# Edge MLP of a four-layer graph network: edge attributes from a three-part bf16 split to unsplit fp32 on the four row groups of TensorE

## Chip, cores and metric

One Trainium2 chip, one of its cores. The metric is the device time of one execution in microseconds (us). The kernel before takes 4524.12 us (median of 3 runs, 4523.55 to 4528.85).

## What is computed

A network of four graph layers over 3125 nodes (128 features) and 50000 edges sorted by target node. The change lies in the edge part of the last layer:

```
ef = jnp.concatenate([x[row], x[col], edge_attr], axis=-1)      # 50000 x (128 + 128 + 32)
h = jax.nn.relu(ef @ W1 + b1)                                   # 256 wide
h = jax.nn.relu(h @ W2 + b2)                                    # 256 wide
edge_out = h @ W3 + b3
aggr = jax.ops.segment_sum(edge_out, col, num_segments=x.shape[0])
```

W1 is used in three pieces: for the source node (its product is a table in DRAM, from which rows are gathered), for the target node (its product is the tile XR, kept as three bf16 parts whose sum is the fp32 value), and for the 32 edge attributes. W3 is applied after the sum over the edges, so the kernel only sums the second relu's result by target node.

## The kernel before

The edges are cut into tiles of 128 edges that share one block of 128 target nodes; four tiles are a quad, and there are 104 quads (QUADS). `mlp_edges` (L1073) runs over the quads in one block of five instruction streams. `in_quads` (L1105) writes out the first four and the last steps and loops over the rest, four steps to an iteration. The order of work is written by hand: each engine's `step` says what it does for which quad, and semaphores tie the engines together.

TensorE's step q (L1190) does, in this order:

- `first(q+1)` (L1150): for each of the four tiles j, three bf16 matmuls of 256 columns (L1158), which pick the target node's row with the 0/1 matrix hot_t, and two bf16 matmuls of 256 columns (L1161) for the edge attributes. It first reads four block numbers into registers (L1100), since L1158's operand address depends on them. Sums go to H1, PSUM banks 0 and 1.
- `second(q)` (L1164): eight fp32 matmuls of 256 columns (L1169), each of which is two instructions in the profile, into H2, banks 4 and 5.
- `turn(q+1)` (L1172): eight transposes of 128 columns (L1177) into T, banks 2 and 3.
- `summed(q-1)` (L1180): eight fp32 matmuls of 128 columns (L1187), two instructions each, into O, banks 6 and 7.

VectorE's step q (L1298): `taken(q-2)` adds O to the accumulator, four instructions (L1296); `added(q+1)` adds the gathered source rows to H1 (L1265), 1024 elements wide; `make_hot_t(q+2)` (L1256, L1258); `rest_parts(q+2)` (L1271); `make_hot(q)` (L1281); `low_parts(q+2)` (L1277); `shifted(q)` adds the bias to H2 (L1288). ScalarE's step q: `high_parts(q+2)` (L1219), `middle_parts(q+2)` (L1223), the relu of T for quad q+1 (L1232), the relu of quad q (L1236). GpSimd gathers the source rows with four indirect DMAs a quad (L1144), into four buffers. SyncE loads, a quad at a time, the targets (L1125, 128 KB) and the four tiles of edge attributes (L1130, 64 KB each).

The edge attributes e (32 numbers) come from DRAM four times over, on 128 partitions: copies 0 and 1 are turned into the bf16 high part, copy 2 into the middle part, copy 3 into the low part. L1219 rounds all four copies to bf16, L1271 subtracts for copies 2 and 3, L1223 rounds what is left, L1277 subtracts again for copy 3. The weights are split alike, once, by GpSimd at the end of `quad_lists` (L1400 to L1416), which runs long before, ahead of the third layer. Two bf16 matmuls over 128 rows then give the product of the split values.

`first(q)` waits for `ea_split` (L1277 of this quad), `hot_t_done` and `h1_added` (L1265 of quad q-1, which frees H1). `turn(q)` waits for `h1_added` of its quad and for `h1_done` (L1232) of the quad before, which frees T.

The third layer (`gine_edges`, L938) already uses fp32 matmuls over 32 rows for the same attributes, four tiles on partitions 0-31, 32-63, 64-95 and 96-127, with their sums in four banks (L1004, 128 columns each).

Of the kernel before, what the change touches and what calls it, by code (L numbers as in the profile page):

```python
# [20 lines left out]
BF16 = mybir.dt.bfloat16  # L21
# [61 lines left out]
def build(nc, t):  # L83

    with ExitStack() as ctx:
# [3 lines left out]
        def sem(name):  # L89
            return ctx.enter_context(nc.semaphore(name))  # L90
# [62 lines left out]
        wrow_all = sb("wrow", [P, 2, GROUP_EDGES], BF16)  # L153
        wrow = wrow_all[0:SPLIT * SPLIT, :, :]
# [918 lines left out]
        def mlp_edges(target):  # L1073
# [14 lines left out]
            ea_hi, ea_rest, ea_mid, ea_split = (sem(f"mlp_ea_{k}") for k in ("hi", "rest", "mid", "split"))  # L1088
            rest = sm[:, 1, :]
            ea_parts = neg  # L1090
# [28 lines left out]
            with nc.Block() as block:  # L1119
                @block.sync  # L1120
                def _(sp):
                    def load(q, r):
# [26 lines left out]
                def _(e):  # L1149
                    def first(q, r):  # L1150
                        s = r % 2
                        blocks = parts_of(mybir.EngineType.PE, q, SUBS)
                        e.wait_ge(ea_split, q + 1)
                        e.wait_ge(hot_t_done, q + 1)
                        wait(e, h1_added, q)
                        for j in range(SUBS):
# [3 lines left out]
                            for k in range(2):  # L1160
                                last = e.matmul(H1[:, j, :], ea_parts[:, s, j * P:(j + 1) * P], edge_w[k], start=False, stop=(k == 1))  # L1161
# [28 lines left out]
                    def step(q, r, k):  # L1190
                        if is_quad(q + 1):
                            first(q + 1, (r + 1) % 4)
# [21 lines left out]
                def _(a):  # L1214
                    def high_parts(q, r, turn):
                        s = r % 2
                        a.wait_ge(ea_in[s], ea_before + 16 * SUBS * (turn + 1))
                        wait(a, h1_ready, q - 1)
                        a.activation(ea_parts[:, s, :], ea_all[:, s, :], ACT.Copy).then_inc(ea_hi, 1)  # L1219

                    def middle_parts(q, r):
                        a.wait_ge(ea_rest, q + 1)
                        a.activation(ea_parts[2 * EDGE_D:, r % 2, :], rest[2 * EDGE_D:, :], ACT.Copy).then_inc(ea_mid, 1)  # L1223

                    def step(q, r, k):
                        if is_quad(q + 2):
# [12 lines left out]
                    high_parts(0, 0, 0)  # L1239
                    middle_parts(0, 0)  # L1240
# [5 lines left out]
                def _(v):  # L1246
# [19 lines left out]

                    def rest_parts(q, r):
                        s = r % 2
                        v.wait_ge(ea_hi, q + 1)
                        wait(v, ea_split, q)  # L1270
                        v.tensor_tensor(rest[2 * EDGE_D:, :], ea_all[2 * EDGE_D:, s, :], ea_parts[2 * EDGE_D:, s, :], ALU.subtract).then_inc(ea_rest, 1)  # L1271

                    def low_parts(q, r):
                        low = ea_parts[3 * EDGE_D:, r % 2, :]
                        v.wait_ge(ea_mid, q + 1)
                        v.wait_ge(ea_rest, q + 1)
                        v.tensor_tensor(low, rest[3 * EDGE_D:, :], low, ALU.subtract).then_inc(ea_split, 1)  # L1277
# [20 lines left out]
                    def step(q, r, k):  # L1298
# [9 lines left out]
                        if is_quad(q + 2):  # L1308
                            low_parts(q + 2, (r + 2) % 4)
# [4 lines left out]
                    rest_parts(0, 0)  # L1314
                    low_parts(0, 0)
# [4 lines left out]

        edge_w = [wrow_all[:, k, 0:HID] for k in range(2)]
# [40 lines left out]
        def quad_lists():  # L1362
# [8 lines left out]
            edge_w_split = sem("edge_w_split")  # L1371
            w_rest = pm[:, 0, 0:HID]
            w_hi, w_mid, w_lo = (pm[:, 1, k * P:(k + 1) * P].bitcast(BF16) for k in range(SPLIT))
# [7 lines left out]
            def pool_also(pool):  # L1381
# [18 lines left out]
                n = [0]  # L1400

                def step(ins):
                    n[0] += 1
                    ins.then_inc(edge_w_split, 1)
                    pool.wait_ge(edge_w_split, n[0])
# [498 lines left out]
```

## Time and profile before

| | |
|---|---|
| median of 3 runs | 4524.12 us (4523.55 to 4528.85) |
| the profiled execution | 4522.14 us, span of its instructions 4520.3 us |
| edge MLP, about | 3510 to 4425 us of the span |
| busy over the whole span | PE 76%, PEld 59%, DVE 59%, ACT 36%, POOL 63% |

PE is TensorE's matmuls, PEld its weight loads, DVE VectorE, ACT ScalarE, POOL GpSimd, SPq and PEq the instruction queues of SyncE and TensorE. In a row of the timeline, the first number is the start in us from the span's beginning, the second the time from the start of the group's first instruction to the end of its last, xN the number of instructions; in square brackets the idle time of the engine before it and what ended it. Matmuls overlap: one of 256 columns lasts about 0.27 us, but in an unbroken stream the next one starts 0.11 us after it. "Issue" is time for which the profile shows no other engine to wait for. The granted clock (PEclk) is 1.00 at 2.4 GHz and 0.50 at 1.2 GHz.

### The profile page before, as it was taken

How to read it: one execution, taken by the hardware profiler on the slowest of the kernel's cores; microseconds unless marked ns; L12 is line 12 of the kernel's file. 1: busy time of each engine (PE TensorE's matmuls, PEld its weight loads, DVE VectorE, ACT ScalarE, POOL GpSimd, SP SyncE). 2: the span in 40 equal slices, each digit the busy share in tenths (PEclk: the TensorE clock that was granted, in tenths of full speed). 3: DMA queues.
4: the chain of work that ended last, by engine and by line, in shares of the span. 5: the costliest groups of instructions: out<-in, count | busy, mean ns of one | idle time of the engine just before them, and what ended most of it. 6: DMA issues, size and time to landing. Idle time of an engine off the chain costs nothing. (4 is left out here: it accounts for less than half of the span.)

```text
span 4520.3 us, 91957 instructions
## 1 busy us (share of the span) xinstructions
PE 3424.3 (76%) x20700; PEld 2666.3 (59%) x20793; DVE 2652.9 (59%) x6184; ACT 1615.5 (36%) x3137; POOL 2825.8 (63%) x2944
## 2 busy tenths in 40 slices
PE   6999999967777755555655555555556799999997
PEld 3777777745555534444444444444444688898894
DVE  5888888866666653333333333333334788888885
ACT  3666666645555531111211111211113333333334
POOL 4555555537777758888678888588884444444440
PEclk7999999979999965555555555655556899999998
DMA  3333333313223212222122222122221333333330
GB/s 113 92 100 100 99 99 100 101 48 80 80 80 80 79 50 59 58 58 59 47 68 59 58 59 59 55 60 58 59 59 48 108 110 110 106 110 109 106 101 15
DMA packets 293253, 349.80 MB, mean 77 GB/s; under 512 B 63537, under 2 KB 236756, under 8 KB 292916
## 3 DMA queue, kind: packets, MB, share of 16 engines
q0 software_dynamic: 98528, 229.12, 17.9%
q1 hardware_dynamic: 140481, 92.05, 7.5%
q10 hardware_dynamic: 54162, 27.77, 2.2%
q8 instruction: 24, 0.39, 0.0%
q14 instruction: 58, 0.47, 0.0%
HBM read 332.61 MB, written 16.07 MB: 77 GB/s over the span
## 5 line engine op out<-in xcount | busy, mean ns | idle before, releaser
L988 POOL DMA_INDIRECT gath<-source_rows_narrow,gine_idx x1176 | 1136.7, 967 | 386.2 <-issue 316.1
L1038 DVE TENSOR_TENSOR vs<-psum,gath 128x512 f32<-128x512 f32 x366 | 253.1, 692 | 1027.7 <-SPq L973 954.0
L1004 PE MATMUL psum<-gine_lin,ea 32*128 32x128 f32 x2928 | 288.4, 483 | 749.3 <-DVE vs L1038 721.7
L1144 POOL DMA_INDIRECT gath<-source_rows,idx_all x416 | 430.3, 1034 | 509.5 <-DVE vs L1265 352.8
L760 POOL DMA_INDIRECT gath<-source_rows,idx_all x488 | 465.1, 953 | 377.2 <-PE psum L807 262.3
L1004 PEld LDWEIGHTS psum<-gine_lin,ea 32*128 32x128 f32 x2928 | 183.8, 297 | 849.9 <-DVE vs L1038 778.7
L760 POOL DMA_INDIRECT gath<-source_rows_narrow,idx_all x488 | 462.8, 948 | 206.1 <-issue 136.6
L790 PE MATMUL psum<-lk,att_b 128*128 128x512 f32 x732 | 375.2, 619 | 113.8 <-DVE lk L885 113.2
L1068 ACT ACTIVATE pm<-vs 128x512 f32<-128x512 f32 x186 | 117.2, 630 | 811.1 <-DVE vs L1038 806.6
L807 PEld LDWEIGHTS psum<-gath,pt 128*128 128x128 f32 x2928 | 365.1, 192 | 36.8 <-DVE zsum L918 1.8
L1013 PE MATMUL psum<-hot,pm 128*128 128x128 f32 x1488 | 363.4, 421 | 20.4 <-ACT pm L1068 19.4
L1169 PE MATMUL psum<-weight_all,pm 128*128 128x256 f32 x1664 | 377.2, 380 | 0.0
L1068 ACT ACTIVATE sm<-vs 128x512 f32<-128x512 f32 x180 | 113.4, 630 | 716.8 <-DVE vs L1038 637.0
L807 PE MATMUL psum<-gath,pt 128*128 128x128 f32 x2928 | 366.4, 275 | 0.9 <-ACT pt L844 0.8
L1013 PE MATMUL psum<-lk,sm 128*128 128x128 f32 x1440 | 358.2, 427 | 1.0 <-ACT sm L1068 1.0
L1013 PEld LDWEIGHTS psum<-hot,pm 128*128 128x128 f32 x1488 | 312.0, 310 | 64.4 <-DVE ACC L1047 45.8
L885 DVE SCALAR_TENSOR_TENSOR lk<-vs 128x512 f32<-128x512 f32 x366 | 253.5, 693 | 159.5 <-DVE vs L881 149.5
L1013 PEld LDWEIGHTS psum<-lk,sm 128*128 128x128 f32 x1440 | 308.4, 316 | 42.7 <-ACT sm L1068 21.7
L1169 PEld LDWEIGHTS psum<-weight_all,pm 128*128 128x128 f32 x1664 | 308.7, 191 | 39.0
L820 ACT ACTIVATE vs<-psum 128x512 f32<-128x512 f32 x366 | 205.4, 595 | 288.9 <-PE psum L772 288.9
L844 ACT ACTIVATE pt<-psum 128x512 f32<-128x512 f32 x366 | 205.5, 595 | 268.6 <-PE psum L799 261.7
L894 DVE CUSTOM_DVE_ANT_0 sm<-psum,neg 128x512 f32<-128x512 f32 x366 | 245.0, 687 | 92.7 <-PE psum L790 91.7
(243 smaller groups left out, 6412.2 us busy)
## 6 DMA issues: line engine op xcount, KB each, us to landing
rel<-rel_rows SPq DMA_DIRECT2D x244, 128.0 KB
ea<-in_edge_attr_tiles SPq DMA_DIRECT2D x416, 64.0 KB
ea<-in_edge_attr ACTq DMA_DIRECT2D x366, 64.0 KB
gath<-source_rows_narrow,gine_idx POOLq DMA_INDIRECT x1176
gath<-source_rows,idx_all POOLq DMA_INDIRECT x904
rel<-quad_rel_rows SPq DMA_DIRECT2D x104, 128.0 KB
gath<-source_rows_narrow,idx_all POOLq DMA_INDIRECT x488
source_rows<-ACC SPq DMA_DIRECT2D x12, 512.0 KB, 2.9
```

The lines of the kernel that those rows point to most:

```text
L760: pool.indirect_dma_start(out=gath[:, i % 4, j, 0:width], out_offset=None, in_=dram, in_offset=bass.IndirectOffsetOnAxis(ap=idx_all[:, i, ...
L790: e.matmul(S[h], att_b[:, att[h], :], lk[:, h, :], start=True, stop=True).then_inc(s_ready, 1)
L807: last = e.matmul(O[h], pt[:, h, j, :], gath[:, s4, j, h * D:(h + 1) * D], start=(j == 0), stop=(j == SUBS - 1))
L885: v.scalar_tensor_tensor(lk[:, h, :], vs[:, h, :], 0.2, vs[:, h, :], ALU.mult, ALU.max).then_inc(leaked, 1)
L894: v.tensor_tensor_reduce(out=sm[:, h, :], in0=S[h], in1=neg[:, s, :], scale=1.0, scalar=-4 * MASK, op0=ALU.subtract, op1=ALU.max, accum_ou ...
L988: pool.indirect_dma_start(out=ring[:, g % RING, j, :], out_offset=None, in_=table1, in_offset=bass.IndirectOffsetOnAxis(ap=gine_idx[:, g, ...
L1004: last = e.matmul(E[:, j, :], ea[rows, s, :], gine_lin[rows, layer, :], start=True, stop=True)
L1013: last = e.matmul(O[s4], pms[s4][:, j * P:(j + 1) * P], hots[s4][:, j, :], start=(j == 0), stop=(j == SUBS - 1))
L1038: v.tensor_tensor(vs[:, s, :].rearrange("p (j d) -> p j d", j=SUBS), E, ring[:, bass.ds(slot, 1), :, :].rearrange("p a j d -> p (a j) d"), ...
L1068: a.activation(pms[s4], vs[:, s, :], ACT.Relu).then_inc(gi["msg"], 1)
L1144: pool.indirect_dma_start(out=gath[:, q % 4, j, :], out_offset=None, in_=table, in_offset=bass.IndirectOffsetOnAxis(ap=quad_idx[:, q, j:j ...
L1169: last = e.matmul(H2[:, j, :], h1[:, h, j * P:(j + 1) * P], w2[h], start=(h == 0), stop=(h == 1))
```

## The change

The edge attributes are loaded once, tile j on partitions 32j to 32j+31, 16 KB each, and are used in fp32 as they are. Their matmul is over 32 rows, on row group j of the array, 256 columns wide, with the fp32 weights, four to a quad (eight instructions, since an fp32 matmul is two), after all twelve matmuls with XR. The four steps of the split on ScalarE and VectorE and the split of the weights on GpSimd go. H1 and T are laid out anew: tile j has bank j, its first half for H1 and its second half for T, so `first` now waits for `h1_done` of the quad before in place of `h1_added`. ScalarE's relu reads T in the new order and writes h1 as before, through another view. SyncE's load of the attributes waits for `h1_ready` (first of the quad two before) in place of `ea_hi` and `ea_rest`. TensorE itself waits for the attributes' DMA, between the two groups of matmuls.

```diff
-            H1 = psum[:, 0:2, :].rearrange("p a n -> p (a n)").rearrange("p (j d) -> p j d", d=HID)
-            T = psum[:, 2:4, :].rearrange("p a n -> p (a n)").rearrange("p (h n) -> p h n", h=2)
+            H1 = psum[:, 0:SUBS, 0:HID]
+            T = psum[:, 0:SUBS, HID:2 * HID].rearrange("p j (h n) -> p j h n", h=2)
...
+            ea_tiles = ea_all[:, :, 0:P]
+            h1_by_tile = pm[:, :, :].rearrange("p h (j n) -> p j h n", j=SUBS)
...
-                        wait(sp, ea_hi, q - 1)
-                        wait(sp, ea_rest, q - 1)
+                        wait(sp, h1_ready, q - 1)
                         for j in range(SUBS):
-                            sp.dma_start(ea_all[:, s, j * P:(j + 1) * P],
+                            sp.dma_start(ea_tiles[EDGE_D * j:EDGE_D * (j + 1), s, :],
...
-                    def first(q, r):
+                    def first(q, r, turn):
                         s = r % 2
                         blocks = parts_of(mybir.EngineType.PE, q, SUBS)
-                        e.wait_ge(ea_split, q + 1)
                         e.wait_ge(hot_t_done, q + 1)
-                        wait(e, h1_added, q)
+                        wait(e, h1_done, q)
                         for j in range(SUBS):
                             for k in range(SPLIT):
                                 e.matmul(H1[:, j, :], hot_t[...], XR[...], start=(k == 0), stop=False)
-                            for k in range(2):
-                                last = e.matmul(H1[:, j, :], ea_parts[:, s, j * P:(j + 1) * P], edge_w[k], start=False, stop=(k == 1))
+                        e.wait_ge(ea_in[s], ea_before + 16 * SUBS * (turn + 1))
+                        for j in range(SUBS):
+                            rows = slice(EDGE_D * j, EDGE_D * (j + 1))
+                            last = e.matmul(H1[:, j, :], ea_tiles[rows, s, :], edge_w1[rows, :], start=False, stop=True)
                         last.then_inc(h1_ready, 1)
...
-                                last = e.transpose(T[:, h, j * P:(j + 1) * P], h1e[:, j, h * D:(h + 1) * D], ident)
+                                last = e.transpose(T[:, j, h, :], h1e[:, j, h * D:(h + 1) * D], ident)
...
-                            high_parts(q + 2, (r + 2) % 4, 2 * k + (r + 2) // 2)
-                            middle_parts(q + 2, (r + 2) % 4)
...
-                            a.activation(h1[:, :, :], T, ACT.Relu).then_inc(h1_done, 1)
+                            a.activation(h1_by_tile, T, ACT.Relu).then_inc(h1_done, 1)
...
-                            rest_parts(q + 2, (r + 2) % 4)
...
-                            low_parts(q + 2, (r + 2) % 4)
...
-                step(pool.tensor_copy(w_hi, edge_w1[:, :]))
-                step(pool.tensor_tensor(w_rest, edge_w1[:, :], w_hi, ALU.subtract))
-                step(pool.tensor_copy(w_mid, w_rest))
-                step(pool.tensor_tensor(w_lo, w_rest, w_mid, ALU.subtract))
-                pool.memset(edge_w[1], 0.0).then_inc(edge_w_split, 1)
...
-                    pool.tensor_copy(edge_w[to][rows, :], part[rows, :]).then_inc(edge_w_split, 1)
```

## Rows read from the trace of the kernel before

**Rows 1.** Busy time of each engine by stretch of the span (also clock, DMA share, GB/s).

```profile
3600.00:3800.00 200.00, 198.04 (x1426) 179.52 (x1425) 168.28 (x261) 77.06 (x96) 97.41 (x95) 1.00 0.39 110
```

**Rows 2.** Timeline of TensorE over one quad's step.

```profile
3907.30 0.54 PE L1158 MATMUL psum<-XR,hot_t 128*128 x3
3907.67 0.38 PE L1161 MATMUL psum<-wrow,neg 128*128 128x256 bf16 x2
3907.89 0.49 PE L1158 MATMUL psum<-XR,hot_t 128*128 x3
...
3909.52 3.62 PE L1169 MATMUL psum<-weight_all,pm 128*128 128x256 f32 x16
3912.98 1.04 PE L1177 MATMUL psum<-consts,vs 128*128 128x128 f32 x8
3913.85 1.95 PE L1187 MATMUL psum<-hot,TMP 128*128 128x128 f32 x16
3916.13 0.41 PE L1158 MATMUL psum<-XR,hot_t 128*128 x2 [0.33 <-issue]
```

**Rows 3.** Timeline of VectorE, ScalarE and SyncE's queue around the same step.

```profile
3905.14 1.90 SPq L1130 DMA_DIRECT2D ea<-in_edge_attr_tiles  x4
...
3905.70 1.03 ACT L1232 ACTIVATE pm<-psum 128x1024 f32<-128x1024 f32 x1 [0.58 <-PE psum L1177]
...
3907.61 2.12 DVE L1296 TENSOR_TENSOR ACC<-ACC,psum 128x256 f32 x4 [0.45 <-PE psum L1187]
...
3909.78 1.23 DVE L1265 TENSOR_TENSOR vs<-psum,gath 128x1024 f32<-128x1024 f32 x1
```

**Rows 4.** Timeline, third layer: one group of four fp32 matmuls over 32 rows.

```profile
1738.71 0.50 PE L1004 MATMUL psum<-gine_lin,ea 32*128 32x128 f32 x8 [0.62 <-DVE vs L1038]
```

**Rows 5.** The same instructions as a group, 1738.5 to 1739.5 us: ns min/median/max.

```profile
L1004 PE MATMUL psum<-gine_lin,ea x8: 270/321/372, 1738.7 to 1738.9; 32*128 32x128 f32 x8
```

**Rows 6.** The same line from 2500 to 2560 us, at clock 0.50.

```profile
L1004 PE MATMUL psum<-gine_lin,ea x104: 416/496/578, 2503.1 to 2556.6; 32*128 32x128 f32 x104
```

**Rows 7.** Timeline of the second layer's XR: 3-row and 128-row matmuls in turn.

```profile
966.23 0.28 PE L482 MATMUL psum<-bias_rows,ones_rows 3*128 3x128 bf16 x1
...
966.44 0.80 PE L480 MATMUL psum<-weight_all,XT 128*128 128x128 f32 x2
967.16 0.10 PEld L482 LDWEIGHTS psum<-bias_rows,ones_rows 3*128 3x128 bf16 x1 [0.23 <-issue]
```

**Rows 8.** Timeline, second layer: a 9-row matmul between 128-row ones.

```profile
1209.41 0.38 PE L780 MATMUL psum<-wrow,we_parts 9*128 9x512 bf16 x1
1209.73 0.82 PE L782 MATMUL psum<-hot_t,XR 128*128 128x512 bf16 x3
```

**Rows 9.** Busy time of each engine by stretch, for the clock of two stretches.

```profile
966.00:974.00 8.00, 8.00 (x28) 4.92 (x26) 2.58 (x4) 2.23 (x4) 6.17 (x7) 0.50 0.21 59
1738.50:1739.50 1.00, 0.50 (x8) 0.31 (x8) 0.45 (x2) 0.63 (x1) 0.94 (x1) 1.00 0.20 66
```

**Rows 10.** Timeline at the end of the stage that splits the weights.

```profile
1649.46 3.02 POOL L1415 COPY wrow<-pm 32x256 bf16<-32x256 bf16 x6
...
1635.38 15.96 SPq L290 DMA_DIRECT2D source_rows_narrow<-TMP  x7
```

**Rows 11.** Timeline of the first quads of the edge MLP.

```profile
3538.68 0.35 DVE L1256 TENSOR_SCALAR hot_t<-rel,consts 128x512 bf16<-128x512 bf16 x1
...
3542.01 0.82 PE L1158 MATMUL psum<-XR,hot_t 128*128 x3 [15.58 <-DVE neg L1277]
...
3546.57 1.22 DVE L1265 TENSOR_TENSOR vs<-psum,gath 128x1024 f32<-128x1024 f32 x1 [4.71 <-PE psum L1161]
...
3551.02 0.82 PE L1158 MATMUL psum<-XR,hot_t 128*128 x3 [2.08 <-DVE neg L1277]
...
3560.38 0.49 PE L1158 MATMUL psum<-XR,hot_t 128*128 x3
3560.58 1.03 ACT L1232 ACTIVATE pm<-psum 128x1024 f32<-128x1024 f32 x1 [1.43 <-PE psum L1177]
```

More of the change, by code:

```diff
@@ L152, in build @@
         rel = sb("rel", [P, 2, GROUP_EDGES], BF16)
-        wrow_all = sb("wrow", [P, 2, GROUP_EDGES], BF16)
-        wrow = wrow_all[0:SPLIT * SPLIT, :, :]
+        wrow = sb("wrow", [SPLIT * SPLIT, 2, GROUP_EDGES], BF16)
         gath = sb("gath", [P, 4, SUBS, 2 * D])
@@ L1083, in mlp_edges @@
             count_turned, count_copied, count_summed, count_done = (sem(f"mlp_count_{k}") for k in ("turned", "copied", "summed", "done"))
-            H1 = psum[:, 0:2, :].rearrange("p a n -> p (a n)").rearrange("p (j d) -> p j d", d=HID)
-            T = psum[:, 2:4, :].rearrange("p a n -> p (a n)").rearrange("p (h n) -> p h n", h=2)
+            H1 = psum[:, 0:SUBS, 0:HID]
+            T = psum[:, 0:SUBS, HID:2 * HID].rearrange("p j (h n) -> p j h n", h=2)
             H2 = psum[:, 4:6, :].rearrange("p a n -> p (a n)").rearrange("p (j d) -> p j d", d=HID)
             O = psum[:, 6:8, :].rearrange("p a n -> p (a n)").rearrange("p (j h n) -> p j h n", j=SUBS, h=2)
-            ea_hi, ea_rest, ea_mid, ea_split = (sem(f"mlp_ea_{k}") for k in ("hi", "rest", "mid", "split"))
-            rest = sm[:, 1, :]
-            ea_parts = neg
+            ea_tiles = ea_all[:, :, 0:P]
             h1e = vs[:, :, :].rearrange("p a n -> p (a n)").rearrange("p (j d) -> p j d", d=HID)
             h1 = pm
+            h1_by_tile = pm[:, :, :].rearrange("p h (j n) -> p j h n", j=SUBS)
             h2a = TMP[:, 0:8, :].rearrange("p a d -> p (a d)").rearrange("p (j d) -> p j d", d=HID)
@@ L1191, in step @@
                         if is_quad(q + 1):
-                            first(q + 1, (r + 1) % 4)
+                            first(q + 1, (r + 1) % 4, 2 * k + (r + 1) // 2)
                         if is_quad(q):
@@ L1214, in _ @@
                 def _(a):
[L1215 to L1223, printed above, removed]
                     def step(q, r, k):
-                        if is_quad(q + 2):
-                            high_parts(q + 2, (r + 2) % 4, 2 * k + (r + 2) // 2)
-                            middle_parts(q + 2, (r + 2) % 4)
                         if is_quad(q + 1):
@@ L1238, in _ @@
                     target.scalar(a)
-                    high_parts(0, 0, 0)
-                    middle_parts(0, 0)
                     in_quads(a, step)
@@ L1265, in added @@
                         v.tensor_tensor(h1e, H1, gath[:, r, :, :], ALU.add).then_inc(h1_added, 1)
[L1267 to L1277, printed above, removed]
                     def make_hot(q, r):
@@ L1313, in _ @@
                     make_hot_t(0, 0, 0)
-                    rest_parts(0, 0)
-                    low_parts(0, 0)
                     in_quads(v, step)
@@ L1318, in _ @@
                     v.tensor_copy(stat[:, 0, :], psum[:, 2, 0:NODE_BLOCKS]).then_inc(count_done, 1)
-        edge_w = [wrow_all[:, k, 0:HID] for k in range(2)]
         def quad_places():
@@ L1370, in quad_lists @@
             rel_b = rel[0:QUADS, 0, :]
-            edge_w_split = sem("edge_w_split")
-            w_rest = pm[:, 0, 0:HID]
-            w_hi, w_mid, w_lo = (pm[:, 1, k * P:(k + 1) * P].bitcast(BF16) for k in range(SPLIT))
             def sp_also(sp):
@@ L1399, in pool_also @@
                 pool.dma_start(quad_rel_rows, rel_b).then_inc(rel_stored, 16)
[L1400 to L1405, printed above, removed]
-                step(pool.tensor_copy(w_hi, edge_w1[:, :]))
-                step(pool.tensor_tensor(w_rest, edge_w1[:, :], w_hi, ALU.subtract))
-                step(pool.tensor_copy(w_mid, w_rest))
-                step(pool.tensor_tensor(w_lo, w_rest, w_mid, ALU.subtract))
-                pool.memset(edge_w[1], 0.0).then_inc(edge_w_split, 1)
-                pool.wait_ge(edge_w_split, 5)
-                for k, (to, at, part) in enumerate(((0, 0, w_hi), (0, 1, w_mid), (0, 2, w_hi), (0, 3, w_hi), (1, 0, w_lo), (1, 2, w_mid))):
-                    rows = slice(EDGE_D * at, EDGE_D * (at + 1))
-                    pool.tensor_copy(edge_w[to][rows, :], part[rows, :]).then_inc(edge_w_split, 1)
-                pool.wait_ge(edge_w_split, 11)
                 pool.wait_ge(rel_stored, 16)
@@ L1881 @@
         "edge_weight": padded(a["edge_weight1"][:, 0], 0).reshape(GROUPS, GROUP_EDGES),
-        "edge_attr_tiles": np.tile(padded(a["edge_attr_32"], 0).reshape(TILES, P, EDGE_D).transpose(0, 2, 1), (1, P // EDGE_D, 1)),
+        "edge_attr_tiles": padded(a["edge_attr_32"], 0).reshape(TILES, P, EDGE_D).transpose(0, 2, 1),
         "edge_attr": padded(a["edge_attr_32"], 0).reshape(GROUPS, SUBS, P, EDGE_D).transpose(0, 1, 3, 2).reshape(GROUPS, SUBS * EDGE_D, P),
```

1 line of the change is left out of this document (removed).

## Prediction, made before the changed kernel ran

> **What bounds the kernel now.** I read the table by stretches first. In the middle of the edge MLP TensorE's matmuls are busy for 198 of 200 us at the full granted clock, VectorE for 168, GpSimd for 97, ScalarE for 77 [rows 1]. So the question is what the change does to TensorE's stream; work taken from the others counts only where they hold TensorE up.
>
> The timeline of one step gives that stream [rows 2]. `first` starts at 3907.30, `second` at 3909.52, `turn` at 3912.98, `summed` at 3913.85, the next `first` at 3916.13: 2.22, 3.46, 0.87 and 2.28 us, the last with 0.33 us in which nothing came. Those 0.33 stand at the back edge of the loop, once in four quads, and none of it is a wait for the split of the attributes. A stage's length is its instruction count times a spacing: in `second` 16 instructions in 3.46 us, 0.216 each for 256 columns in fp32. In `first` there are 20 bf16 instructions of 256 columns. Three in a row take 0.49 us from first start to last end and two take 0.38, so one more costs 0.11. Only the first three of a quad stand wider: 0.37 us to the fourth, 0.123 each, against 0.32 for the three from 3907.89 on. These are the L1158 ones, whose address comes from a register; I read it as TensorE's queue handing them out one by one, while a quad's first have no lead.
>
> The rest has room. ScalarE's relu of T ends at 3905.70 + 1.03 = 3906.73, 0.57 before `first` starts [rows 2, 3]. VectorE ends its four sums at 3909.73 and begins `added` at 3909.78, when H1 is ready; it ends at 3911.01, 1.97 before `turn` wants it [rows 2, 3].
>
> **What the change removes.** Per quad: eight bf16 matmuls of 0.11, 0.87 us of TensorE; two VectorE and two ScalarE instructions of 512 columns, which hide behind TensorE today and so give nothing. After them VectorE has less to do than before in every step, and what is late next is TensorE again. On GpSimd the weight split goes; its last copies end at 1652.48, while SyncE's last store is only issued at 1651.34 and has yet to land before the stage can end [rows 10]. I give it 0 (between -1 and 0).
>
> **What it adds on TensorE, per quad.** Eight fp32 instructions over 32 rows and 256 columns, two rounds on four row groups. The third layer has the same form with 128 columns. At clock 1.00 its eight take 0.50 us from first start to last end [rows 4, 9]; the eight one after another would take 7 x 0.108 + 0.27 = 1.03. The longest lasts 372 ns, the shortest 270 [rows 5]. That fits a first weight load of 0.10 in the open, two rounds 0.11 apart, 0.02 for the four starts and 0.27 for the last (0.10 + 0.11 + 0.02 + 0.27 = 0.50). So four row groups do run side by side, and a round of 256 columns costs 0.216: two make 0.43, plus 0.02.
>
> The price of going between 128-row and 32-row matmuls is in two places. A 3-row matmul in turn with fp32 ones over 128 rows, at clock 0.50 [rows 7, 9]: from its start at 966.23 to the next load at 966.44 is 0.21, of which 128 bf16 columns at 1.2 GHz stream for 0.107, so 0.10 on the way back. From there to the next 3-row load at 967.16 is 0.72: two fp32 instructions of 128 columns stream 0.43, their first load stands open for 0.16 (the longest less the shortest at this clock, 578 - 416 ns, [rows 6]), 0.13 is left for the way in. No weight load starts ahead: TensorE's load row shows 0.23 us idle. At clock 1.00 a 9-row matmul of 512 columns starts at 1209.41 and the 128-row one 0.32 later; the next of these come at (0.82 - 0.38) / 2 = 0.22, so the way back costs 0.10 at full clock too [rows 8]. I take 0.12 in and 0.10 back, and an open load of 0.10 after each: 0.42 a quad. Bounds: 0, were all of it hidden, and 0.60, were both ways and both loads as at half the clock (0.13, 0.16, 0.10, 0.16, and a rounding up).
>
> One rule speaks against the change: by the Trainium skill, TensorEngine Tiling (Array Packing), Key Properties, a change of tiling mode (not of tile alone) drains TensorE. By this rule two drains a quad are paid, and the trace agrees with 0.12 and 0.10; without the rule the sum below would be 0.22 a quad less.
>
> **What it moves.** The twelve XR matmuls now come in one row, with no L1161 between them. Today the L1161 pairs let the queue catch up; without them the 0.123 to 0.13 of a quad's first three [rows 2] may hold for all twelve. Bounds 12 x 0.108 = 1.30 and 12 x 0.13 = 1.56; I take 1.50, nearer to the row that has no lead. TensorE's own wait for the attributes' DMA comes after them; its target is worked out from a register, an instruction of the same kind as those in between, and I hide it under the way in. SyncE's four loads today go out at 3905.14 and take 1.90 to issue [rows 3]; the new wait lets them go when `first` of two quads before ends, near 3909.5, and they are wanted two steps, 16 us, later. The next `rel` load queues behind them and moves by under half a us, with as much to spare. They carry 16 KB in place of 64.
>
> `first` now waits for the relu of T, not for `added`. In a full step the relu is 0.57 us early, and `summed` lies between. Behind that wait are `second`, `turn` and `summed`, so a late relu would move everything; I take 0. The relu of T itself becomes a read of four half banks of the same 1024 elements, at 1.03.
>
> Sum for `first`: 1.50 + 0.12 + 0.10 + 0.43 + 0.02 + 0.10 + 0.10 = 2.37, against 2.22: **+0.15 us**. For the 102 quads in the full stream +15.3.
>
> **The start.** The first `first` begins at 3542.01, after the split of quad 0; its other input, hot_t, ended at 3539.03 [rows 11]. Put 0.15 behind it, it starts at 3539.18, 2.8 earlier. At clock 0.50 it is some 0.5 shorter (eight instructions of 0.213 go, 0.85 of rounds and some 0.4 of changes come), so `added(0)` moves from 3546.57 to 3543.2. Then 1.22, the transposes 1.04 and the relu 1.03, with three hand-overs: 3546.8 for the second `first`, against 3551.02, which waited for the split of quad 1: -4.2. The third `first` follows the transposes at once today (3560.38), before the relu at 3560.58 has run; in this step there is no `summed` yet, so the new wait costs 3561.61 + 0.15 - 3560.38 = 1.4. Start: -2.8 (between -5 and 0, as the clock falls).
>
> **Total:** +15.3 - 2.8 = +12.5. The profiled execution took 4522.14, 2.0 under the median: 4534.6 for it, some 4537 for a median. A measurement of this kernel can tell about 0.2%, 9 us, from no change.
>
> **Rivals.**
>
> *The row groups win (faster).* Place: between the last XR matmul and `second`. If the loads of the new mode are fetched ahead and nothing drains, and the twelve keep 0.108, `first` is 1.30 + 0.43 + 0.02 = 1.75: -0.47 a quad, -48 and -3 at the start, 4473. For it: the clean 0.50 for eight in the third layer [rows 4]. Against: rows 7 and 8, where no load is early. It decides once pacing and changes together cost under 0.41 where I reckon 0.62 (0.20 and 0.42): then `first` is 0.06 shorter than today and the sum, with the start, is -9. Chance 0.11, and 0.04 more for part of it.
>
> *The pacing does not hold (no change).* With 1.30 for the twelve `first` is 2.17 to 2.20: -0.03 a quad, -3 and -3: 4518 to 4522. For it: all later threes stand at 0.11 today. Against: they have a lead then. Chance 0.20.
>
> *The relu is late (slower by more).* From 0.57 us later on, each 0.1 costs 10 us. It might come from ScalarE's order or a slower read across four banks; 0.3 past the point gives 4567. ScalarE loses two instructions, which speaks against. Chance 0.05.
>
> *The row groups don't run together,* so that the change doesn't do what it says: 8 x 0.216 = 1.73 in place of 0.43, +133: 4670. Against: rows 4. Its one difference is that sums are added to what H1 holds, not begun. Chance 0.04.
>
> *My forecast:* 0.56, by itself 4528 to 4550, some 0.10 of it within 9 us of no change.
>
> Slower: 0.46 + 0.05 + 0.04 = 0.55. No change: 0.10 + 0.20 = 0.30. Faster: 0.11 + 0.04 = 0.15. The range takes in the second rival and half of the gap to the first (4505), and upwards the 0.60 for changes and 1.56 for pacing, (0.18 + 0.06) x 102 = +24 more (4560); it leaves out the first rival and the last two.
>
> **What would show it.** In the profile after: `first` from its first L1158 to the first L1169 at 2.37 plus an open load, which shows as L1169's first matmul longer than its others; the twelve at 0.124, end of the last to the first 32-row load some 0.1 with TensorE's load row idle; eight 32-row matmuls in about 0.7 from first start to last end; `second`, `turn` and `summed` at 3.46, 0.87 and 1.79 as before; VectorE at about 6.3 us a quad, waiting for TensorE before L1265 or L1288; the second `first` some 8 us behind the first, no longer 9. The forecast is wrong if the twelve take 1.30, if loads start before the last XR matmul has ended, or if TensorE sits idle before L1158 for the relu in each step.

## The result, and the profile after

| | before | after |
|---|---|---|
| median of the runs, us | 4523.84 (4522.45 to 4529.80, 6 runs) | 4543.34 (4543.04 to 4546.34, 6 runs) |
| the profiled execution, us | 4522.14 | 4543.88 |
| its span, us | 4520.3 | 4542.1 |
| mean granted clock of TensorE | 0.797 | 0.795 |

The changed kernel is slower: ratio 1.0041, with an interval of 1.0028 to 1.0054, or +19.5 us. The forecast was 4537 in a range of 4505 to 4560. Three single executions in these rounds took 5259 to 6786 us (two of the kernel before, one of experiment 2), and the ratios leave them out, while the medians have them in.

TensorE is still the engine without room. The first fence is the middle stretch of the edge MLP as in [rows 1] (us, then busy us and instructions of PE, PEld, DVE, ACT and POOL; clock, DMA share, GB/s). VectorE is at 131 of 200 us instead of 168, ScalarE at 45 instead of 77, and TensorE stays at 198 with fewer instructions, 1400 for 1426:

```profile
3600.00:3800.00 200.00, 198.20 (x1400) 166.56 (x1399) 131.37 (x210) 45.49 (x47) 88.54 (x93) 1.00 0.31 84
```

The timeline of one step, which answers to [rows 2, 3]:

```profile
3908.13 1.02 ACT L1217 ACTIVATE pm<-psum 128x1024 f32<-128x1024 f32 x1 [6.48 <-PE psum L1175]
...
3909.72 1.67 PE L1154 MATMUL psum<-XR,hot_t 128*128 x12
...
3910.03 2.12 DVE L1267 TENSOR_TENSOR ACC<-ACC,psum 128x256 f32 x4 [1.55 <-PE psum L1185]
...
3911.32 0.71 PE L1159 MATMUL psum<-edge_w,ea 32*128 32x256 f32 x8
3911.97 3.72 PE L1167 MATMUL psum<-weight_all,pm 128*128 128x256 f32 x16
...
3912.16 1.23 DVE L1248 TENSOR_TENSOR vs<-psum,gath 128x1024 f32<-128x1024 f32 x1
...
3915.53 1.04 PE L1175 MATMUL psum<-consts,vs 128*128 128x128 f32 x8
```

`first` now takes 3911.97 - 3909.72 = 2.25 us, `second` 3915.53 - 3911.97 = 3.56. Before they were 2.22 and 3.46: the step is 0.13 longer. The twelve L1154 matmuls last 1.67 from first start to last end; one lasts 0.28, so their starts stand (1.67 - 0.28) / 11 = 0.126 apart. The eight of 32 rows take 0.71. `second` is 0.10 longer for its first weight load, which stands open. The weight loads of the same step:

```profile
3909.72 1.49 PEld L1154 LDWEIGHTS psum<-XR,hot_t 128*128 128x128 bf16 x12
3911.32 0.31 PEld L1159 LDWEIGHTS psum<-edge_w,ea 32*128 32x128 f32 x8
3911.97 3.32 PEld L1167 LDWEIGHTS psum<-weight_all,pm 128*128 128x128 f32 x16 [0.33 <-issue]
```

No load of L1167 starts before the last 32-row matmul has streamed: 0.33 us of idle load row. The first matmul behind it shows this as its length. In the group of these matmuls over two steps (ns, min/median/max) the longest is 483 where before it was 382:

```profile
L1167 PE MATMUL psum<-weight_all,pm x32: 379/379/483, 3903.5 to 3915.3; 128*128 128x256 f32 x32
```

Who waits for whom, from 3565 to 4430 (us in total, times, longest):

```profile
DVE ACC L1267 <- PE psum L1185: 163.1, 100, 2.0
DVE TMP L1259 <- PE psum L1167: 63.3, 100, 0.8
PEld psum L1167 <- issue: 33.5, 101, 0.3
...
PE psum L1154 <- issue: 6.6, 23, 0.4
PE psum L1154 <- ACT pm L1217: 1.3, 1, 1.3
```

VectorE waits for TensorE in each step. TensorE waits for the relu of T once, in the third quad, and never in the steady stream.

**Where the 21.8 us between the two spans lie.** The edge MLP begins with the memset of its accumulator; in the trace before it starts at 3533.3, after at 3543.0:

```profile
L1231 DVE MEMSET ACC<- x1: 5392/5392/5392, 3543.0 to 3543.0; 128x6400 f32 x1
```

From there to the end it is 987.0 before and 999.1 after, +12.1. The edge MLP is not all of that: from the memset to the end of its last sums it is 901.3 before and 910.1 after, **+8.9 us in the edge MLP** by the unrounded times, and what follows it takes 85.8 before and 88.9 after, **+3.1 behind it**. The diff changes nothing behind it. Over all the traces of this study that last stretch takes 85.8 to 90.5 us, the shortest at a granted clock of 0.86 and the longest at 0.78; here the clock is 0.86 before and 0.81 after. The other **+9.8 us stand ahead of it**, where the diff has nothing but the removed split of the weights and the smaller buffer and input. The third layer's gathers are the group that grew there. From the first to the last it took 3449.0 - 1654.4 = 1794.6 us before; the same rows give 3460.9 - 1657.2 = 1803.7 after, 9.1 more. First of before (L988), then of after (L987), duration in ns as min/median/max:

```profile
L988 POOL DMA_INDIRECT gath<-source_rows_narrow,gine_idx x1176: 943/947/1459, 1654.4 to 3449.0; - x196
```

```profile
L987 POOL DMA_INDIRECT gath<-source_rows_narrow,gine_idx x1176: 947/952/1437, 1657.2 to 3460.9; - x196
```

The page gives them a mean of 967 ns before and 974 after: 1176 x 7 ns = 8.2 us. VectorE, whose L1037 adds the gathered rows, has room: the page has it idle for 1036.6 us before that line. GpSimd has none: the gaps between its gathers, with what it does in them, add up to 658.9 us before and 659.0 after (658.5 to 659.7 over fourteen traces), so the stretch grows by what the gathers themselves last.

The start of the edge MLP, TensorE's timeline, which answers to [rows 11]:

```profile
3548.96 2.74 PE L1154 MATMUL psum<-XR,hot_t 128*128 x12 [12.76 <-DVE hot_t L1239]
...
3556.48 2.74 PE L1154 MATMUL psum<-XR,hot_t 128*128 x12 [1.31 <-ACT pm L1217]
3559.15 0.71 PE L1159 MATMUL psum<-edge_w,ea 32*128 32x256 f32 x8
3559.79 3.72 PE L1167 MATMUL psum<-weight_all,pm 128*128 128x256 f32 x16
3563.35 1.04 PE L1175 MATMUL psum<-consts,vs 128*128 128x128 f32 x8
3565.70 1.77 PE L1154 MATMUL psum<-XR,hot_t 128*128 x12 [1.31 <-ACT pm L1217]
```

Counted from the memset, the first three `first`s begin at 5.9, 13.5 and 22.7 us; before they began at 8.8, 17.8 and 27.1.

### The profile page after: what moved, and what is told of

Same layout as the page of the kernel before. It is cut to its first block and busy times, and to the rows that moved or that the text cites. A ratio compares the mean times of both kernels' runs of the same rounds, so it can differ in the third digit from the quotient of the medians.

```text
span 4542.1 us, 91093 instructions
## 1 busy us (share of the span) xinstructions
PE 3447.4 (76%) x20700; PEld 2629.2 (58%) x20793; DVE 2498.2 (55%) x5976; ACT 1484.0 (33%) x2929; POOL 2799.9 (62%) x2933
## 5 line engine op out<-in xcount | busy, mean ns | idle before, releaser
L987 POOL DMA_INDIRECT gath<-source_rows_narrow,gine_idx x1176 | 1145.5, 974 | 391.6 <-issue 316.1
L1037 DVE TENSOR_TENSOR vs<-psum,gath 128x512 f32<-128x512 f32 x366 | 253.2, 692 | 1036.6 <-SPq L972 962.9
L1141 POOL DMA_INDIRECT gath<-source_rows,idx_all x416 | 401.5, 965 | 544.5 <-DVE vs L1248 389.0
L759 POOL DMA_INDIRECT gath<-source_rows,idx_all x488 | 463.7, 950 | 376.9 <-PE psum L806 262.0
L1167 PE MATMUL psum<-weight_all,pm 128*128 128x256 f32 x1664 | 386.8, 385 | 0.0
L1167 PEld LDWEIGHTS psum<-weight_all,pm 128*128 128x128 f32 x1664 | 307.6, 190 | 71.8 <-issue 34.2
L1217 ACT ACTIVATE pm<-psum 128x1024 f32<-128x1024 f32 x104 | 106.5, 1024 | 697.2 <-PE psum L1175 697.2
```

The lines of the kernel that those rows point to most:

```text
L759: pool.indirect_dma_start(out=gath[:, i % 4, j, 0:width], out_offset=None, in_=dram, in_offset=bass.IndirectOffsetOnAxis(ap=idx_all[:, i, ...
L987: pool.indirect_dma_start(out=ring[:, g % RING, j, :], out_offset=None, in_=table1, in_offset=bass.IndirectOffsetOnAxis(ap=gine_idx[:, g, ...
L1037: v.tensor_tensor(vs[:, s, :].rearrange("p (j d) -> p j d", j=SUBS), E, ring[:, bass.ds(slot, 1), :, :].rearrange("p a j d -> p (a j) d"), ...
L1141: pool.indirect_dma_start(out=gath[:, q % 4, j, :], out_offset=None, in_=table, in_offset=bass.IndirectOffsetOnAxis(ap=quad_idx[:, q, j:j ...
L1167: last = e.matmul(H2[:, j, :], h1[:, h, j * P:(j + 1) * P], w2[h], start=(h == 0), stop=(h == 1))
```

## The experiments

Where a distance of quads is given, it is the mean distance between the starts of two `first`s, from the fourth of them to the 101st: **8.467 before, 8.600 after**. Each ratio is to the kernel before on the same chip.

**1. The new banks and the new wait alone.** The kernel before with H1 and T in four shared banks:

```diff
-            H1 = psum[:, 0:2, :].rearrange("p a n -> p (a n)").rearrange("p (j d) -> p j d", d=HID)
-            T = psum[:, 2:4, :].rearrange("p a n -> p (a n)").rearrange("p (h n) -> p h n", h=2)
+            H1 = psum[:, 0:SUBS, 0:HID]
+            T = psum[:, 0:SUBS, HID:2 * HID].rearrange("p j (h n) -> p j h n", h=2)
...
-                        wait(e, h1_added, q)
+                        wait(e, h1_done, q)
```

> The kernel before with only the new layout of H1 and T (one bank per tile, the relu through the new view) and with first waiting for h1_done; the attributes stay split. My theory (TensorE's stream in first sets the step, the new wait has 0.5 us of room): the steady quad stays at 8.47 us, the third first waits 1.4 us once for the relu, total 4525 to 4527. Rival (the relu is late in each step): 0.1 us and more a quad, above 4534.

Measured: 4533.0 against 4526.26, ratio 1.0011 (1.0001 to 1.0021). The distance is 8.468, so the banks and the wait cost nothing in the stream. The third `first` is at 28.9 us after the memset, against 27.1 and 26.8 in two traces of the kernel before: +1.9, the wait for the relu in the start. The other 5 us are in no part that this edit touches. In the profiled execution the stretch behind the edge MLP is 90.5 us, against 85.8 and 87.4 in the two traces of the kernel before, at a granted clock of 0.78 against 0.86 and 0.84: 3 to 5 us lie there. Whether that is chance is left open; two executions of the kernel before also differ by 6.4 us ahead of the MLP (its memset at 3533.3 and at 3539.7). The expected 4525 to 4527 was missed.

**2. The order of the matmuls alone.** As 1, with all twelve XR matmuls ahead of the eight bf16 ones:

```diff
                                          start=(k == 0), stop=False)
+                        for j in range(SUBS):
                             for k in range(2):
```

> The same as e_layout, and the eight bf16 matmuls of the split attributes come after all twelve XR matmuls. No 32-row matmul, no change of mode. My theory (TensorE's queue hands out the XR matmuls one by one at 0.125 us, and static matmuls in between let it catch up): the twelve take 0.125 each, first to second 2.38 us in place of 2.22, so +15 us over e_layout, 4540. Rival (pacing is only in a quad's first three, the rest of the loss in the changed kernel is the mode changes): first stays at 2.22, 4526.

Measured: 4547.59, ratio 1.0047 (1.0031 to 1.0064). The distance is 8.616, +0.148 over experiment 1, for the same instructions. TensorE's timeline:

```profile
3912.57 1.66 PE L1159 MATMUL psum<-XR,hot_t 128*128 x12
3914.06 1.04 PE L1163 MATMUL psum<-wrow,neg 128*128 128x256 bf16 x8
3914.94 3.62 PE L1171 MATMUL psum<-weight_all,pm 128*128 128x256 f32 x16
```

Twelve start 0.125 apart, the eight behind them (1.04 - 0.27) / 7 = 0.110. So the order by itself makes all of the loss in the stream; the 32-row matmuls give back 8.616 - 8.600 = 0.016 of it.

**3. The 32-row matmuls first.** The change, with its eight ahead of the twelve:

```diff
+                        e.wait_ge(ea_in[s], ea_before + 16 * SUBS * (turn + 1))
+                        for j in range(SUBS):
+                            rows = slice(EDGE_D * j, EDGE_D * (j + 1))
+                            e.matmul(H1[:, j, :], ea_tiles[rows, s, :], edge_w1[rows, :], start=True, stop=False)
                         for j in range(SUBS):
                             for k in range(SPLIT):
-                                         start=(k == 0), stop=False)
+                                         start=False, stop=(k == SPLIT - 1))
```

> The changed kernel with the eight 32-row matmuls ahead of the twelve XR matmuls (start and stop flags moved accordingly). My theory: while the array works on the attributes the queue gets ahead, so the twelve run at 0.11 each, and the way back opens onto a bf16 load of 0.01 in place of an fp32 one of 0.10: first to second about 2.06 in place of 2.38, -32 us against the changed kernel, 4511. Rival (the change of mode holds the queue too, so no lead is won): the twelve stay at 0.125 and only the 0.09 of the load goes, 4534.

Measured: 4511.33, ratio 0.9966 (0.9953 to 0.9979), 32 us under the change. The distance is 8.275:

```profile
3903.55 0.71 PE L1155 MATMUL psum<-edge_w,ea 32*128 32x256 f32 x8
3904.19 1.49 PE L1158 MATMUL psum<-XR,hot_t 128*128 x12
3905.51 3.62 PE L1167 MATMUL psum<-weight_all,pm 128*128 128x256 f32 x16
...
3912.13 0.71 PE L1155 MATMUL psum<-edge_w,ea 32*128 32x256 f32 x8 [0.34 <-issue]
```

The twelve stand at (1.49 - 0.27) / 11 = 0.111 here, and `second` is back at 3.46: behind the 32-row matmuls comes a bf16 load now and not an fp32 one. `first` is 1.97 and `summed` 1.88 instead of 1.79, which puts the way into the 32-row form at 0.09. Two things are gained at once here, the pacing of the twelve and the open fp32 load; experiments 8 and 10 take them apart.

**4. The attributes' size in DRAM.** The change with the input four times over, as before:

```diff
-                                         t["edge_attr_tiles"][bass.ds(tiles[j], 1), :, :].rearrange("a k e -> (a k) e")).then_inc(ea_in[s], 16)
+                                         t["edge_attr_tiles"][bass.ds(tiles[j], 1), 0:EDGE_D, :].rearrange("a k e -> (a k) e")).then_inc(ea_in[s], 16)
```

> The changed kernel, but its input of edge attributes keeps the size that it had before (four copies in DRAM, of which one is read), so every DRAM tensor lies as before. It asks where the 9.8 us come from by which the changed kernel reaches its edge MLP later (3543.0 against 3533.3). Theory A (the place of the tensors in DRAM makes gathers slower): the edge MLP starts at 3533 to 3535 again and the total is about 4535. Theory B (it is something else: code length, the GpSimd stage that is gone, chance): start stays at 3543, total 4543.

Measured: 4548.16, ratio 1.0046 (1.0028 to 1.0064), memset at 3546.6, gathers at a median of 955 ns. What lies where in DRAM is not the cause of the 9.8 us.

**5. The kernel before, once more,** unchanged, for the chance between executions.

> The kernel before once more, for how much of the differences ahead of the edge MLP is chance between executions. If it is chance: its edge MLP starts anywhere from 3533 to 3543. If the code decides: 3532 to 3535, with a third layer's group (gathers of 947 ns median) as before.

Measured: 4528.33, memset at 3539.7, gathers 940/946/1447 ns. So 6.4 of the 9.8 us are within what one and the same kernel shows; the gathers' median stays at 946 to 947.

**6. GpSimd's split of the weights put back** into the change, its result unused, with the scratch buffer declared as before:

```diff
+                step(pool.tensor_copy(w_hi, edge_w1[:, :]))
+                step(pool.tensor_tensor(w_rest, edge_w1[:, :], w_hi, ALU.subtract))
...
+                pool.wait_ge(edge_w_split, 11)
                 pool.wait_ge(rel_stored, 16)
```

> The changed kernel with what it removed ahead of the edge MLP put back: GpSimd's split of the weights into the tile on 128 partitions (the result is not used). Theory A (one of these two makes the third layer's gathers quicker, 947 ns in kernels that have the split, 952 to 955 in those that lack it): gathers back at 947, edge MLP starts 3534 to 3538, total 4536. Theory B (the gathers' time goes by something else): gathers at 952 or more, total 4543 to 4547.

Measured: 4541.89 against 4528.02, ratio 1.0029 (1.0017 to 1.0042), distance 8.601, memset at 3538.7, gathers back at 947 ns. The total is 6 us above the expected 4536. GpSimd's timeline shows what the split delays at that place, and it is nothing. With it:

```profile
1652.32 3.00 POOL L1382 COPY wrow<-pm 32x256 bf16<-32x256 bf16 x6
1657.22 1.06 POOL L988 DMA_INDIRECT gath<-source_rows_narrow,gine_idx  x1 [1.89 <-POOLq L283]
```

Without it, in the trace of the change:

```profile
1649.29 0.69 POOL L1360 DMA_DIRECT2D quad_rel_rows<-rel  x1 [0.30 <-POOL rel L1358]
1657.25 1.05 POOL L987 DMA_INDIRECT gath<-source_rows_narrow,gine_idx  x1 [7.27 <-POOLq L282]
```

The first gather starts at 1657.2 in both (over seven traces with the split and seven without, at 1655.9 and 1656.8 on average); what differs is how long each of the 1176 takes.

**7. The scratch buffer's declaration alone,** without the split:

```diff
-        wrow = sb("wrow", [SPLIT * SPLIT, 2, GROUP_EDGES], BF16)
+        wrow_all = sb("wrow", [P, 2, GROUP_EDGES], BF16)
+        wrow = wrow_all[0:SPLIT * SPLIT, :, :]
```

> The changed kernel with the tile wrow declared on 128 partitions again, as before, and nothing else; GpSimd splits no weights. e_weight_split had both, and its third layer's gathers were back at 947 ns. Theory A (the declaration moves other tiles in SBUF, and gathers depend on it): 947, edge MLP starts 3536 to 3541, total 4537 to 4542. Theory B (GpSimd's eleven instructions are the cause, by its code's place or what it did before): gathers at 952 to 955, start 3542 to 3548.

Measured: 4542.5 against 4529.16, ratio 1.0034 (1.002 to 1.0048), memset at 3544.3, gathers 955 ns. The declaration is not the cause.

**8. Register loads a stage earlier.** The change with `summed` of the quad before moved to the head of the step and the addresses of `first` read ahead of it, so that TensorE's queue works them out while matmuls are still running:

```diff
                     def step(q, r, k):
+                        blocks = parts_of(mybir.EngineType.PE, q + 1, SUBS) if is_quad(q + 1) else None
+                        if is_quad(q - 2):
+                            summed(q - 2, (r - 2) % 4)
                         if is_quad(q + 1):
-                            first(q + 1, (r + 1) % 4, 2 * k + (r + 1) // 2)
+                            first(q + 1, (r + 1) % 4, 2 * k + (r + 1) // 2, blocks)
...
-                        if is_quad(q - 1):
-                            summed(q - 1, (r - 1) % 4)
```

> The changed kernel, with TensorE's reading of the four block numbers moved ahead of summed, and summed of the quad before to the start of the next step (same order of matmuls). My theory: the queue reads them while 16 or more pairs are still to run, so it has a lead when first begins: the twelve XR matmuls run at 0.11, and the 0.33 us at the loop's back edge go too. First to second 2.20, a quad 8.30 in place of 8.60: -30 us against the changed kernel, 4514. Rival (0.124 is what such a matmul costs whatever the lead): only the back edge goes, 0.1 a quad, 4533.

Measured: 4511.42, ratio 0.9962 (0.9948 to 0.9976), distance 8.267. The twelve are at (1.47 - 0.27) / 11 = 0.109:

```profile
3912.52 1.47 PE L1153 MATMUL psum<-XR,hot_t 128*128 x12
3913.92 0.71 PE L1158 MATMUL psum<-edge_w,ea 32*128 32x256 f32 x8
3914.57 3.72 PE L1166 MATMUL psum<-weight_all,pm 128*128 128x256 f32 x16
```

`first` is 2.05 and `second` still 3.56. The distance got shorter by 0.33, 0.21 of it in `first`; the rest, 0.12, is the pause at the loop's back edge, which is gone. The rows call it 0.33, counted from the end of the last matmul; from start to start it is 2.28 - 1.79 = 0.49, once in four quads.

**9. The same early loads in the kernel before,** with no other edit.

> The kernel before (split attributes) with the block numbers read early, as in e_early. My theory: only a quad's first three XR matmuls are paced there (0.05 us) and the back edge costs 0.12 a quad on average, so 8.30 in place of 8.47: -17 us, 4509. So with both read early the fp32 form gives 8.27 to this one's 8.30, a gain of 3 us. Rival (the split form gains as much as the fp32 form did, 0.33 a quad): 4492.

Measured: 4513.86, ratio 0.9969 (0.9957 to 0.998), distance 8.299. With a lead in both kernels, the change's own form is worth 8.299 - 8.267 = 0.03 us a quad, 3 us in all.

**10. Both improvements of the change,** early loads and the 32-row matmuls first (the edits of 3 and 8 together).

> Both: block numbers read early, and the 32-row matmuls ahead of the XR ones. The pacing is already gone in e_edges_first; what is new is the back edge of the loop (0.33 us and more in four quads) and any other lateness of the queue at a quad's start. My theory: a quad takes 8.16 in place of 8.28, -12 us against e_edges_first, 4499. Rival (the reading of the numbers then holds TensorE up elsewhere): 4511 or more.

Measured: 4505.93, ratio 0.9951 (0.9935 to 0.9968). The distance is 8.177, close to the 8.16 expected, and 0.09 under experiment 8: with a lead in both, that is what the place of the 32-row matmuls is worth alone; the time is 7 us over the expected one, and its memset is at 3548.3, gathers at 955 ns: the part ahead of the MLP again.

**11. Experiment 10 with GpSimd's split put back** as in 6.

> e_early_edges_first with GpSimd's split of the weights put back (its result is not used), since the two kernels that have that split and a 32-row or a bf16 form alike show gathers of 947 ns and those without it 952 to 955. Steady quad 8.18 as in e_early_edges_first, edge MLP at 3534 to 3541 in place of 3548: 4498 to 4502. Rival (the two parts don't add up, because the place of the gathers' code is what counts and moves again): gathers at 955, 4506.

Measured: **4493.85 against 4528.73, ratio 0.9924 (0.991 to 0.9937)**, the fastest complete kernel of this study and faster than both; 4498 to 4502 was expected. The distance is 8.177 as in 10, the memset at 3536.5. Its gathers:

```profile
L988 POOL DMA_INDIRECT gath<-source_rows_narrow,gine_idx x1176: 940/945/1462, 1653.5 to 3453.7; - x196
```

Its timeline and its middle stretch, TensorE at 200.00 of 200:

```profile
3908.62 1.95 PE L1185 MATMUL psum<-hot,TMP 128*128 128x128 f32 x16
3910.50 0.71 PE L1155 MATMUL psum<-edge_w,ea 32*128 32x256 f32 x8
3911.15 1.48 PE L1158 MATMUL psum<-XR,hot_t 128*128 x12
3912.47 3.62 PE L1167 MATMUL psum<-weight_all,pm 128*128 128x256 f32 x16
```

```profile
3600.00:3800.00 200.00, 200.00 (x1470) 174.55 (x1467) 137.31 (x223) 47.33 (x49) 91.89 (x98) 1.00 0.33 88
```

**12. The change without the attributes' matmuls,** so without their part of the first product, and with eleven small GpSimd memsets in the place of the split. TensorE's wait for the attributes' DMA stays, now ahead of the twelfth XR matmul:

```diff
-                        for j in range(SUBS):
-                            rows = slice(EDGE_D * j, EDGE_D * (j + 1))
-                            last = e.matmul(H1[:, j, :], ea_tiles[rows, s, :], edge_w1[rows, :], start=False, stop=True)
...
+                                if j == SUBS - 1 and k == SPLIT - 1:
+                                    e.wait_ge(ea_in[s], ea_before + 16 * SUBS * (turn + 1))
...
+                for k in range(11):
+                    pool.memset(hot_t[0:1, k % 2, k:k + 1], 0.0).then_inc(edge_w_split, 1)
```

> Two separate questions. First, the changed kernel without the 32-row matmuls, the attributes' part of the first product being left out (their DMA and TensorE's wait for it stay, ahead of the twelfth XR matmul): theory, they cost 0.85 us a quad in all, so a quad takes 7.75 in place of 8.60; rival, they cost the 0.45 of their two rounds, 8.15. Second, GpSimd gets eleven tiny memsets (one element each) at the place where the split of the weights stood: if the number of instructions ahead of the third layer's gathers is what counts, gathers at 947 ns and the edge MLP at 3534 to 3541; if the split's own work or time is, 952 to 955 and 3542 to 3550.

Measured: 4474.5 in one execution, distance 7.921: leaving the eight out saves 8.600 - 7.921 = 0.68 us a quad, between the two theories:

```profile
3899.98 1.78 PE L1156 MATMUL psum<-XR,hot_t 128*128 x12 [0.33 <-issue]
3901.60 3.71 PE L1165 MATMUL psum<-weight_all,pm 128*128 128x256 f32 x16
...
3909.33 0.10 PEld L1156 LDWEIGHTS psum<-XR,hot_t 128*128 128x128 bf16 x1 [0.16 <-issue]
```

`second`'s first matmul is long here too (475 ns), with no 32-row matmul ahead of it. What is late ahead of it is the twelfth: its weight load comes 0.16 us after the one before has ended, and over 97 quads it starts 0.211 behind the eleventh where the others stand 0.124 to 0.133 apart. The one thing that sets it apart is the wait for the DMA ahead of it. So 0.09 a quad for this wait and about 0.08 for the open load behind it are in the 7.921, and in the change both lie under the change of form; without them the distance would be 7.921 - 0.17 = 7.75 and 8.600 - 7.75 = 0.85 would be saved, which is the first theory's sum. That is an estimate, and no run has the twelve without the wait. It doesn't make the change of form cheaper: experiment 8 has the long first matmul (483 ns) in a queue with a lead. The gathers are at 952 ns and the memset at 3545.4: eleven small instructions do not do what the split does.

## Why the prediction was right, and where it was not

**Right: the sum for `first`, and its two halves.** It had the pacing of the twelve at 1.50 in place of 1.35, +0.15, and the exchange of eight bf16 matmuls for the 32-row ones with their changes at 0.87 against 0.87, 0. Measured, each by itself: +0.148 (experiment 2 over 1) and -0.016 (the change over experiment 2). Over the stream that is 102 x 0.133 = +13.6; from the third `first` to the last of `summed` the trace has +13.3, where I had +15.3. The way in was taken at 0.12 and measured 0.09, the open load behind it fits at 0.10. (The sign "2.37 plus an open load" counts that load twice, since the 2.37 has both; the trace has 2.25 to the first L1167 and 0.10 behind it.)

By the Trainium skill, TensorEngine Tiling (Array Packing), Key Properties, a change of tiling mode drains TensorE. The trace agrees: 0.09 us on the way in, with a lead in the queue too (experiment 10), and no load ahead on the way out.

**Right: four row groups run side by side.** Eight one after another would be 8 x 0.216 = 1.73 us, an estimate from the spacing in `second`. In the trace 0.65 pass from their first start to `second`, some 0.55 without the way back of 0.10: 3.1 times faster. The serial rival is out.

The Trainium skill, TensorE: Matmul & The Clock Gate, Measured speedup vs the span model, gives 3.07 for four row tiles of 512 columns. The trace agrees, at 256 columns in fp32 and against that estimate.

**Right: the relu does not hold the stream.** Its wait is there once, for 1.31 us in the third quad (1.4 predicted), and experiment 1 has the stream at 8.468 with the same wait. The relief of VectorE and ScalarE bought nothing, as costed. VectorE's own sum was off: 131.37 of 200 us is 5.65 us a quad, where I had 6.3.

**Right in part: the start.** The first `first` moved by -2.8 and the second by -4.3 (predicted -2.8 and -4.2). The third moved by -4.4, not by -2.8. The step between them was to be 1.4 longer for the relu; from the second `first` to `turn` it is 3563.35 - 3556.48 = 6.87 us against 3559.51 - 3551.02 = 8.49. `first` at clock 0.50 is 0.9 shorter (3.31 for 4.24), where I had reckoned 0.5, and `second` runs wholly at the high clock, 3.56 for 4.25: in the trace of before its first 1.7 us are still at about 0.5. I had carried the first gain only once and the second not at all.

**Wrong: "On GpSimd the weight split goes ... I give it 0 (between -1 and 0)".** Its working looked only at the end of its stage, and there it holds: the first gather starts at the same time with and without. What it missed is the 1176 gathers behind it. Over all fourteen traces, the seven of kernels that hold the split have gathers with a median of 945 to 947 ns and the memset at 3533.3 to 3539.8 (mean 3537.9); the seven that don't have 952 to 955 ns and 3542.0 to 3550.2 (mean 3545.7). The ranges don't overlap, and the means are 7.8 us apart. Clearer still is the stretch from the first gather to the last: 1794.6 to 1800.2 us with the split, 1803.7 to 1806.1 without, 6.9 apart on average. That is the missing term, 7 to 8 us. With it the prediction is 4537 + 8 = 4545, against 4543.34, and that this comes so near is in part luck: the edge MLP was forecast at +12.5 and measured at +8.9, and the +3.1 behind it, which no term had, makes up for that. In the times it is seen clearly in one pair, experiments 10 and 11 (0.9951 and 0.9924, 12 us); in the other, 7 and 6 (1.0034 and 1.0029), it is under what can be told. The cause is bounded and not settled. It isn't DRAM (4), nor the buffer (7), nor the mere number of instructions (12, eleven as in the split). Whether it is the length of GpSimd's program ahead of the gathers, where its code lies, or the kind of those instructions was not tried; nor was the split's own length varied.

**The rivals.** "The pacing does not hold" fell with the twelve at 0.126. "The row groups win" named 0.41 as the sum from which it decides; pacing and changes came to about 0.15 + 0.39 (0.09 and 0.10 for the ways, 0.20 for the loads). With a lead the pacing does go, and the change's form is then 0.03 us a quad ahead (8 against 9), what that rival gave it; the first rival's -0.47 is seen nowhere.

**What bounds the twelve.** Ahead of the first, TensorE's queue loads four values into registers and works out addresses; then come the matmuls whose address is in a register. Experiment 2 shows that their order costs 0.148 with nothing else changed, 8 and 9 that the same matmuls in the same order cost nothing more once the loads are ahead of `summed`. The L1161 pairs of the kernel before, with fixed addresses, were what let the queue catch up between threes: the change took away TensorE's slack in issuing along with the work. That order and place of the loads set the pace is measured; that it is the register in the address which makes such a matmul slow to hand out is my reading, since no run gives the twelve fixed addresses.

## What to carry to other kernels

Count what an instruction costs the queue as well as the array: a dozen matmuls with addresses from registers in a row ran at 0.125 us each where the array needs 0.109, and cheap fixed ones between them, or the register loads one stage earlier, hide that. When small-row matmuls join a stream of full ones, put them where a bf16 load follows them, not an fp32 one; here the same eight instructions at the other end of the stage turned +0.13 us a quad into -0.19. Of those 0.32, 0.09 is the place alone (experiment 10 against 8); the rest is the lead that they give the queue. And a stage that an edit touches "off the path" is to be compared by the durations of what follows it too, not only by when it ends.

## What the runs showed of the hardware that was not expected

- An indirect gather's time on GpSimd (945 to 947 ns against 952 to 955, medians of 1176 each, seven traces a side) depends on what the program holds ahead of it, by a mechanism left open.
- The pause of 0.33 us at the loop's back edge [rows 2] goes when back edge and register loads follow `turn` and stand ahead of `summed`. The branch is there in both, so by itself it costs TensorE nothing where the queue is full; the pause was a queue with nothing to hand out. In the kernel before, with no other edit, early loads alone give 8.467 - 8.299 = 0.17 us a quad, 0.3% of the whole time.
- An open fp32 weight load of 0.10 us comes from two causes that look the same in a row: the change of form (experiment 8, with a lead) and a late matmul just ahead, behind a semaphore wait and without a lead (experiment 12, without the form).
